# An attention and gated low-rank layer on one core: a new layout of a batch's places, a small softmax that subtracts and sums in ScalarE's exponentials, and a gate that writes its mask itself

## The reference

```
xn   = layernorm(x)
q    = (xn Wq^T + bq) * 0.25            # 16 heads of 16
k, v = split(xn Wkv^T + bkv)            # one k and one v of 16, shared by all heads
attn = softmax(q k^T) v ; y1 = attn Wo^T + bo

g      = one-hot of argmax(xn w_gate)   # 6 experts, the first of equals
tok_e  = A_e B_e                        # A_e 100x16, B_e 16x256
p      = softmax(xn tok_e^T / 16)       # 100 columns, only the chosen expert counts
delta  = ((p[1:] (tok_e Wt^T + wt_b)[1:] + xn) Wd^T + wd_b) * scale
y2     = xn + log(exp(delta))           # a sum of 0 is replaced by a tiny number
out    = x + y1 + y2
```

## Time and profile before

| | |
|---|---|
| median of 3 runs | 1049.19 us (1047.77 to 1050.99) |
| profiled execution | 1037.82 us |
| its span, first to last instruction | 1036.0 us |
| TensorE busy | 892.1 us, 86% |
| VectorE busy | 812.0 us, 78% |
| ScalarE busy | 661.6 us, 64% |
| GpSimd busy | 515.6 us, 50% |
| mean granted TensorE clock | 0.937 of full |

### The profile page before, as it was taken

The page is one execution under the profiler, slowest core; times in us unless marked ns, Lnnn a source line. Parts: engine busy times, 40 slices in busy tenths (PEclk is TensorE's granted clock), DMA queues, the critical chain, the costliest instruction groups (busy, mean ns, idle before and its releaser), DMA issues.

```text
span 1036.0 us, 17715 instructions
## 1 busy us (share of the span) xinstructions
PE 892.1 (86%) x5837; PEld 287.0 (28%) x5837; DVE 812.0 (78%) x1523; ACT 661.6 (64%) x1334; POOL 515.6 (50%) x693
## 2 busy tenths in 40 slices
PE   1368988888999999898998898899899989989986
PEld 0223222322233232222223232223223223222222
DVE  5369898878889896888779787878878888877814
ACT  1003776766677685776667677667757767667882
POOL 1457375555557373555547455555636555532400
PEclk9766999989999998999899999989989999998988
DMA  4224144253524353253525326262533625241121
GB/s 121 60 55 67 56 76 97 74 103 93 87 85 91 105 94 89 82 104 94 95 65 90 102 82 110 87 94 67 90 94 81 114 83 104 61 77 52 54 67 37
DMA packets 128209, 86.56 MB, mean 84 GB/s; under 512 B 60279, under 2 KB 112248, under 8 KB 128120
## 3 DMA queue, kind: packets, MB, share of 16 engines
q1 hardware_dynamic: 128120, 85.43, 36.8%
HBM read 39.28 MB, written 33.54 MB: 70 GB/s over the span
## 4 chain that ended last, share of the span: by engine, by line
PE 53%; DMA 15%; DVE 14%; SPq 6%; ACT 4%; issue 4%; POOL 4%; POOLq 0%
PE pO L358 17%; PE pA L340 12%; DMA o_parts<-OTr 7%; DVE M L768 7%; DMA Lc<-o_parts 6%; PE pB L345 5%; SPq L993 5%; PE pA L483 4%; PE pA L412 3%; PE pA L465 3%; ACT P L585 2%; PE pA L452 2%; PE pA L401 2%; ACT OTr L591 2%; POOL KS L870 2%
## 5 line engine op out<-in xcount | busy, mean ns | idle before, releaser
L768 DVE TENSOR_REDUCE M<-pA 128x1 f32<-128x512 f32 x1024 | 644.6, 678 | 85.0 <-PE pA L340 83.2
L585 ACT ACTIVATE P<-pB 128x512 f32<-128x512 f32 x1002 | 556.7, 600 | 236.4 <-PE pB L345 227.5
L340 PE MATMUL pA<-K,Q 48*128 48x512 f16 x1024 | 342.0, 400 | 78.6 <-DVE M L768 66.9
L345 PE MATMUL pB<-Q,K 50*128 50x512 f16 x1002 | 333.8, 397 | 0.3 <-DVE M L768 0.3
L358 PE MATMUL pO<-P,VK 128*32 128x512 f32 x2048 | 287.1, 634 | 10.1 <-ACT P L585 7.9
L340 PEld LDWEIGHTS pA<-K,Q 48*128 48x128 f16 x1024 | 70.3, 95 | 432.8 <-DVE M L768 374.4
L925 POOL TENSOR_TENSOR On<-Op,Rb 128x512 f32<-128x512 f32 x31 | 39.9, 1287 | 178.2 <-DMA Rb<-l_parts 131.9
L876 POOL CAST Qp<-qf 128x512 f16<-128x512 f32 x32 | 19.5, 609 | 131.4 <-DVE qf L724 131.4
L911 POOL TENSOR_SCALAR Cz<-Cx 128x512 f32<-128x512 f32 x32 | 62.1, 1940 | 30.6 <-ACT Cx L567 30.5
L483 PE MATMUL pA<-wo,On 128*128 128x256 f32 x248 | 71.5, 413 | 3.3 <-DVE RL L781 1.9
L774 DVE RECIPROCAL Rc<-Lc 128x32 f32<-128x32 f32 x31 | 10.9, 353 | 79.5 <-DMA Lc<-o_parts 79.5
(11 more groups left out here) (144 smaller groups left out, 810.3 us busy)
## 6 DMA issues: line engine op xcount, KB each, us to landing
o_parts<-OTr SPq DMA_DIRECT2D x62, 256.0 KB, 2.1
Q<-q_pieces SPq DMA_DIRECT2D x90, 128.0 KB, 5.1
X<-in_x SPq DMA_DIRECT2D x16, 512.0 KB, 3.9
q_pieces<-Qp SPq DMA_DIRECT2D x32, 256.0 KB, 2.3
out<-OUT SPq DMA_DIRECT2D x32, 256.0 KB, 3.2
Op<-o_parts SPq DMA_DIRECT2D x31, 256.0 KB
Rb<-l_parts SPq DMA_DIRECT2D x31, 256.0 KB
K<-KS SPq DMA_DIRECT2D x96, 16.0 KB, 1.8
```

The costliest lines, as they stand in the source:

```text
L340: e.matmul(bank1("ab", t)[:, :], Q16[r:r + 48, b % 2, h, 128 * s:128 * s + 128], K16[r:r + 48, b % 3, :], start=True, stop=True).then_inc( ...
L345: e.matmul(bankB(t)[:, :], K16[r:r + 50, b % 3, 128 * i:128 * i + 128], Q16[r:r + 50, b % 2, :, 32 * hh:32 * hh + 32], start=True, stop=Tr ...
L585: e.activation(P[:, u % PR, :], bankB(u + LB)[:, :], ACT.Exp, scale=alpha).then_inc(S("e"))
L768: e.tensor_reduce(M[:, t // 32 % 2, t % 2, t % 32 // 2:t % 32 // 2 + 1], bank1("ab", t)[:, :], AX, ALU.max, negate=True).then_inc(S("mx"))
```

## The change

Three things are changed together. First, SLOT has other places, and with them go three Q buffers instead of two, other DMA shapes for Q and K (k's 16 rows come out of the projection twice, so that one copy carries two of the three pieces), the evictions qf on ScalarE instead of VectorE, and another start: the first batch's tokens are transposed by TensorE, ScalarE makes the high pieces of the weights and issues the first batch's K copies, and the first Q reads go out in two separate places. Second, the small softmax: VectorE writes the negated maximum, four exponentials of 100 columns read the scores in PSUM with it as bias and write their sums; Sd and the sum on VectorE are gone, and the factor 1/16 is in UK's scale. Third, the gate's last comparison writes the 384 mask elements itself; `oh` and GpSimd's cast are gone.

```diff
 SLOT = {
-    "root": -91.4, "refine": -90.2, "norm": -87.2, "pieces": -84.2, "xtd": -74.2,
-    "residual": 2.3, "q0": -57, "qe0": -55.4, "qs0": -53.8, "qw0": -50.2, "uk": -53, "uke": -51.4, "ks": -50.2,
...
+    "root": -91.4, "refine": -90.2, "norm": -87.2, "ph": -82.4, "pl": -79, "xtd": -66.2,
+    "residual": 9.1, "q0": -53, "qe0": -51.4, "qs0": -47.5, "qw0": -45, "uk": -49, "uke": -47.4, "ks": -45.2,
...
-PARTH = {"lr": 66.2, "or": 66.3, "rec": 68.8, "lw": 69.4, "rb": 72.2, "on": 78.3}
+PARTH = {"lr": (82.2, 114.2), "or": (82.3, 114.3), "rec": (88.8, 120.8), "lw": (89.6, 121.4), "rb": (92.4, 124.4),
+         "on": (98.2, 130.3)}
...
-        Q16 = sb("Q16", [128, 2, H, T // 2], F16)
+        Q16 = sb("Q16", [128, 3, H, T // 2], F16)
...
-            "ab": lambda t: (S("mx"), t + 1), "s": lambda b: (S("sd"), b + 1),
+            "ab": lambda t: (S("mx"), t + 1), "s": lambda b: (S("es"), 4 * b + 4),
...
+                for c in range(2):
+                    if due(f"xt{c}", n) is not None:
+                        w.wait_ge(*before2(f"xt{c}", 0))
+                        w.wait_ge(S("id"), 4)
+                        for i in range(4):
+                            w.wait_ge(S("xn"), i + 1)
+                            mm = e.transpose(bank2(f"xt{c}", 0)[:, 128 * i:128 * i + 128], XN[:, i, 128 * c:128 * c + 128],
+                                             idf[:, :])
+                        mm.then_inc(S("xtp"))
...
+                if due("kd", n) == 0:
+                    w.wait_ge(S("kl"), 1)
+                    w.wait_ge(S("kc"), 2)
+                    for a in range(2):
+                        e.dma_start(K16[64 * a:64 * a + 32, 0, :], KS[96:128, 0, :]).then_inc(S("kd"), 16)
+                        e.dma_start(K16[64 * a + 32:64 * a + 48, 0, :], KS[96:112, 1, :]).then_inc(S("kd"), 16)
+
+                for g in range(2):
+                    if (b := due(f"qe{g}", n)) is not None:
+                        w.wait_ge(S(f"q{g}"), b + 1)
+                        w.wait_ge(S("bqs"), 1)
+                        w.wait_ge(S(f"ql{g}"), b)
+                        e.activation(qf[:, g, :], bank1(f"q{g}", b)[:, :], ACT.Identity, scale=scl[:, 5:6],
+                                     bias=bq_s[:, g:g + 1]).then_inc(S(f"qe{g}"))
...
-                    w.wait_ge(S("sd"), b + 1)
+                    w.wait_ge(S("sm"), b + 1)
                     w.wait_ge(S("en"), b)
-                    e.activation(Es[:, :, :], Sd[:, :, :], ACT.Exp, scale=C ** -0.5).then_inc(S("es"))
+                    for i in range(4):
+                        e.activation(Es[:, i, :], bank1("s", b)[:, NL * i:NL * i + NL], ACT.Exp, bias=smx[:, i:i + 1],
+                                     accum_out=sL[:, i:i + 1]).then_inc(S("es"))
...
-                    w.wait_ge(S("mk"), b)
-                    e.tensor_tensor(oh[:, :, :], gw[:, :, :], bc(gm2[:, :], NE), ALU.is_equal).then_inc(S("oh"))
+                    w.wait_ge(S("mkd"), 16 * b)
+                    w.wait_ge(S("mk1"), 1)
+                    e.tensor_tensor(mk[:, :, 0:ER].rearrange("p i (e r) -> p i e r", r=NR), bc(gw[:, :, :], NR),
+                                    bc(bc(gm2[:, :], NE), NR), ALU.is_equal).then_inc(S("mk"))
...
-                    e.tensor_reduce(smx[:, :], s4, AX, ALU.max).then_inc(S("sm"))
-                    w.wait_ge(S("sm"), b + 1)
-                    w.wait_ge(S("es"), b)
-                    e.tensor_tensor(Sd[:, :, :], s4, bc(smx[:, :], NL), ALU.subtract).then_inc(S("sd"))
+                    w.wait_ge(S("es"), 4 * b)
+                    e.tensor_reduce(smx[:, :], s4, AX, ALU.max, negate=True).then_inc(S("sm"))
...
-                if (b := due("qread", n)) is not None:
-                    if b >= 2:
-                        w.wait_ge(S("b"), 64 * (b - 1))
...
+                if (b := due("qread", n)):
+                    w.wait_ge(S("qw_0"), 32 * (b + 1))
+                    w.wait_ge(S("qw_1"), 32 * (b + 1))
+                    if b > 2:
+                        w.wait_ge(S("b"), 64 * (b - 2))
+                    for a in range(2):
+                        for p, pieces in ((0, 2), (32, 1)):
+                            e.dma_start(Q16[64 * a + p:64 * a + p + 16 * pieces, b % 3, :, :],
+                                        qd[b % 2, :, 0:pieces, :, 256 * a:256 * a + 256]
+                                        .rearrange("h k d t -> (k d) h t")).then_inc(S(f"qr_{b % 2}"), 16)
```

More of the change, by code:

```diff
@@ L23 @@
 ER = NE * NR
-U0, K0, V0, WC = C, C + ER, C + ER + D, C + ER + D + 32
-UKW = ER + D
+U0, K0, V0, WC = C, C + ER, C + ER + 2 * D, C + ER + 2 * D + 32
+UKW = ER + 2 * D
 LN_EPS = 1e-5
@@ L119, in slots @@
                 put(name, 16 * g + slot + 4 * (g >= 4 * NB - 4), g)
-        if g % 2 and g < 4 * NB - 2:
-            for name, slot in PARTH.items():
-                put(name, 16 * g + slot + 4 * (g >= 4 * NB - 4), g // 2)
+    for nh in range(2 * NB - 1):
+        for name in PARTH:
+            put(name, 64 * (nh // 2) + (PARTH_LAST[name] if nh == 2 * NB - 2 else PARTH[name][nh % 2]), nh)
     return at
@@ L703, in _ @@
                     e.tensor_tensor(rstd[:, :], y4[:, :], y0[:, :], ALU.mult).then_inc(S("ry"))
-                if due("pieces", n) == 0:
-                    for k in range(2):
-                        w.wait_ge(S("xh0"), k + 1)
-                        e.tensor_tensor(XP[:, 2 * k:2 * k + 2, 1, :], XN[:, 2 * k:2 * k + 2, :],
-                                        XP[:, 2 * k:2 * k + 2, 0, :], ALU.subtract).then_inc(S("xl0"))
+                for c in range(2):
+                    if due(f"xl{c}", n) is not None:
+                        w.wait_ge(S("xh0"), c + 1)
+                        e.tensor_tensor(xT[:, 0, :, 1, c, :], bank2(f"xt{c}", 0)[:, :].rearrange("p (i t) -> p i t", t=128),
+                                        xT[:, 0, :, 0, c, :], ALU.subtract).then_inc(S("xl"))
                 if (b := due("uke", n)) is not None:
@@ L717, in _ @@
                                     ALU.mult, ALU.add).then_inc(S("uke"))
-                for g in range(2):
-                    if (b := due(f"qe{g}", n)) is not None:
-                        w.wait_ge(S(f"q{g}"), b + 1)
-                        w.wait_ge(S("bqs"), 1)
-                        w.wait_ge(S(f"ql{g}"), b)
-                        e.tensor_scalar(qf[:, g, :], bank1(f"q{g}", b)[:, :], scl[:, 5:6], bq_s[:, g:g + 1],
-                                        ALU.mult, ALU.add).then_inc(S(f"qe{g}"))
+                if due("qs0", n) == 0:
+                    w.wait_ge(S("qe0"), 1)
+                    e.tensor_copy(Qp[:, 0, 0, :], qf[:, 0, :]).then_inc(S("qh0"))
+                    w.wait_ge(S("qh0"), 1)
+                    e.tensor_tensor(Qp[:, 0, 1, :], qf[:, 0, :], Qp[:, 0, 0, :], ALU.subtract).then_inc(S("ql0"))
                 if (b := due("gate", n)) is not None:
@@ L872, in _ @@
                 for g in range(2):
-                    if (b := due(f"qs{g}", n)) is not None:
+                    if (b := due(f"qs{g}", n)) is not None and b + g:
                         w.wait_ge(S(f"qe{g}"), b + 1)
-                        w.wait_ge(S(f"qw_{g}"), 16 * b)
+                        w.wait_ge(S(f"qw_{g}"), 32 * b)
                         e.tensor_copy(Qp[:, g, 0, :], qf[:, g, :]).then_inc(S(f"qh{g}"))
@@ new lines, in _ @@
+                        for k in range(2):
+                            e.dma_start(qd[b % 2, 8 * g:8 * g + 8, k], Qp[:, g, k, :]).then_inc(S(f"qw_{g}"), 16)
+                for half, name in enumerate(("qra", "qrb")):
+                    if due(name, n) is not None:
+                        w.wait_ge(S(f"qw_{half}"), 32)
+                        for a in range(2):
+                            for p, pieces in ((0, 2), (32, 1)):
+                                e.dma_start(Q16[64 * a + p:64 * a + p + 16 * pieces, 0, 8 * half:8 * half + 8, :],
+                                            qd[0, 8 * half:8 * half + 8, 0:pieces, :, 256 * a:256 * a + 256]
+                                            .rearrange("h k d t -> (k d) h t")).then_inc(S(("qf", "qr_0")[half]), 16)
```

163 lines of the change are left out of this document (75 added, 88 removed), and 8 rows, old and new, of the table SLOT.

## The result

The changed kernel takes 936.15 us (median of 4 runs, 935.8 to 937.19), the kernel before 1048.48 us on the same chip (4 runs, 1039.02 to 1050.99): a ratio of 0.8945, 95% interval 0.8889 to 0.9001. The profiled execution took 935.8 us. Forecast: 928, range 903 to 972. The kernel before varies from run to run (1025 to 1056 us on one chip of the experiments), and every ratio with its interval compares the fast runs of the two kernels only.

A forecast was written before the change was run, and what follows sets the result against it. No engine was saturated; VectorE's `rec` waits for the row sums and clock falls cost time. Span 1036.0 - 96.5 (batches) - 15 (start) - 1 (tail) = 923.5; 925 profiled with 1.8 around it, plus 3: 928 us, range 903 to 972.

The forecast's parts named there:

- The stall and the clock: VectorE's `rec` waits for Lc vanish, 4.65 us per batch (65.1 in all); TensorE's clock stops falling, 27 us.
- The Q reads: SyncE's queue: `qread` moves to ten places ahead of `ow`; the reads need 8 us or nine places, so clear it.
- VectorE: VectorE's evictions and small operations: net -2.7 us busy per batch, counted as -1.0, bounds 0 and -2.
- ScalarE: ScalarE gains two `qf` and four exponentials for one Es: +2.7 us busy per batch, counted +0.7, bounds 0 and 2.7.
- over 15 us of such waits: Sign that the forecast is wrong: TensorE's waits on ScalarE for a bank grow past 15 us.
- ScalarE becomes the bound: Rival, chance 0.12: ScalarE frees q0's, q1's and the small softmax's banks late, 0.9 us each; period 55, 966 us.
- The period: Time per batch: 57.3 - 4.65 - 1.0 + 0.7 = 52.3 us; fourteen batches -96.5 us.
- Start and tail: Start: mask ready near 30.2, -15 us, bounds -8 and -22. Tail: last batch's places hardly move, -1 us.
- The clock did not fall again: Rival, chance 0.10: TensorE's clock still falls through short idle times; 955 us as often as now, 987 once every batch.
- Slower by On, the guard and `dlog0`: Rival, chance 0.03: `on` waits for Rb ahead of GpSimd's guard, ScalarE's `dlog0` behind; up to 10.4 us a batch, 1074.
- Part of the `rec` wait stays: Rival, chance 0.05: one `rec` in a batch still waits 2 us and the clock falls as now, 983 us.
- Better: Case, chance 0.04: VectorE's whole 2.7 us per batch count, 900 us.

The follow-up runs named there:

- Experiment 1: Kernel before with `rec`, `lw`, `rb` and `on` four places later: 1044.67 us, ratio 1.0136.
- experiment 2: Kernel before with `rec`, `lw`, `rb`, `on` and also `o0` four places later: 965.99 us, ratio 0.934.
- experiment 4: Changed kernel with Q's reads back at place 45.8, still with three Q buffers: 935.26 us, ratio 0.8987.
- experiments 6: Changed kernel with the old small softmax and the old gate, so the layout alone: 921.22 us, ratio 0.8935.
- experiment 7: Changed kernel with one small part undone: old softmax alone 927.13 us, ratio 0.8959; old gate alone 930.65 us, ratio 0.8989.
- experiment 8: Changed kernel, three variants: one of three d-projection products left out, 922.73 us; row maxima over 448 of 512 columns, 928.12; `qf` back on VectorE, 944.38.
- experiment 3: Changed kernel with `rec`, `lw` and `rb` four places earlier: 939.86 us, ratio 0.9112.
- experiment 5: Kernel before with only the new small softmax and the gate that writes the mask, old layout: 1036.15 us, ratio 1.0027.

## Why the prediction was right, and where it was not

**The stall and the clock (step: minus 4.65 per batch, minus 27 for falls).** The state forecast came about: no `rec` wait in the fourteen batches, clock 1.00 for all 742.7 us, batches near 53. The mechanism held for Lc; the attribution did not hold for the rest. The prediction took `rec` to be the stall and gave its disappearance to `rec`'s four places and to Q's. Experiment 1 shows that a later `rec` by itself only hands the stall to `o0`; experiment 2 that `o0`'s move is needed with it in that kernel: from place 3.0 to 7.2 there, to 7.0 in the change (131 to 135 in SLOT), which the prediction does not name. A wait was costed as if removing it ended the matter, when it stood at the head of a chain of two DMA round trips whose other end was due at a fixed place. The sizes were off as well, in opposite ways: the `rec` waits counted 65.1 us, and TensorE's idle time, all causes together, fell by 53.3; the clock counted 27 us, called its upper bound, and TensorE's busy time fell by 32.8.

**The Q reads (step: "`qread` moves from 45.8 to 38.2 ... so they now clear it").** The effect is there, Lc 2.1 us behind `ow`; the cause named is wrong. The new place gives the same order as the old one (experiment 4), and the reads come earlier because they no longer wait 3.6 us a batch for a buffer. The prediction knew of that wait and did not count its end.

**VectorE (step: -2.7 busy, -1.0 counted).** Busy went from 49.1 to 46.8 us in the batches shown, -2.3. What the small softmax and the gate's mask contributed to the period has the wrong sign: +0.75 together (experiments 6 and 7), and some 3 us in batch 0. The gate's error lies in a duration: `oh` was taken at 764 ns, its mean before, so that the mask in its stead seemed free. In the new layout `oh` takes 182 ns and the mask 558. The 764 belonged to `oh`'s neighbour, below.

**ScalarE (step: +2.7 busy, +0.7 counted).** It has 42.7 us per batch where 43.9 were forecast: +1.5 for +2.7. By the lengths of the added instructions, the ones that read the sums included, it would be 2 x 0.77 + 4 x (0.35 + 0.21) - 0.54 = +3.2; rows of neighbours overlap, and busy time counts such a stretch once. `qf` took 772 ns (800 forecast), an exponential 347 (400). By the Trainium skill's sum (ScalarE: Activation LUTs, What ACT_TABLE_LOAD costs) they would have been an estimated 799 and 362; the trace agrees within 30 ns. What was not foreseen is the instruction behind each exponential. The groups of the changed kernel, and one of the four pairs with what TensorE does behind it:

```profile
L574 ACT ACTIVATE qf<-pA,bq_s,scl 128x512 f32<-128x512 f32 x32 | 24.7, 772 | 19.5 <-PE pA L426 19.5
L596 ACT ACTIVATE Es<-pA,smx 128x100 f32<-128x100 f32 x64 | 21.0, 347 | 2.2 <-DVE smx L788 2.2
L596 ACT ACTIVATION_READ_ACCUMULATOR Es<-pA,smx 128x1 f32 x64 | 13.5, 211 | 0.0
```

```profile
558.22 0.34 ACT L596 ACTIVATE Es<-pA,smx 128x100 f32<-128x100 f32 x1
558.45 0.20 ACT L596 ACTIVATION_READ_ACCUMULATOR Es<-pA,smx 128x1 f32 x1
...
559.50 1.10 ACT L627 ACTIVATE P<-pB 128x512 f32<-128x512 f32 x2
...
559.68 0.39 PE L344 MATMUL pA<-K,Q 48*128 48x512 f16 x1 [0.48 <-ACT Es L596]
```

The group holds ScalarE from 558.22 to 559.50, 1.3 us where Es took 0.54, and it holds the bank of `s` too: before, VectorE's subtraction freed that bank; now the last exponential does, and TensorE waits for it once in every batch, 14 times, 6.8 us in all (the 10.9 us of its weight loads in the same list lie over the same moments, 558.90 to 559.68 and 559.20 to 559.68 here). The prediction's sign for the rival, over 15 us of such waits, did not appear. That is the mechanism of the rival "ScalarE becomes the bound" for one of its three banks, and 0.49 us a batch is the likely place of the softmax's 0.4 us, as the wait comes and goes with the four exponentials (experiment 7). The term of +0.7 per batch held in size against the two parts together, but the gain of 1.0 set against it did not come from them. Of the 1.8 us between experiment 2's batch and the layout's (54.1 and 52.3), `qf`'s move to ScalarE has 0.6 by experiment 8; the other 1.2 are not separated: the third Q buffer, fewer issues, and many other places moved together.

**The period.** Forecast 52.3, measured 53.05; fourteen batches -86.0 us instead of -96.5. The miss is the 0.75 above, nearly to the digit, since the layout alone gave 52.3. The rest agrees in part by luck: two attributions in the sum were wrong.

**Start and tail.** -15 forecast, -14.7 measured, which already holds the 3 us that the two small parts cost in batch 0; no run takes the parts of the new start one by one. The second batch's projection at 47.37 lies within the 46 to 49 forecast, the mask was ready at 29.4, near the 30.2. The tail gave -1.3 for -1. The median lies 0.35 us above the profiled execution; 3 had been allowed for.

**The rivals.** The clock did not fall again: 14 batches with their short waits for a bank ran at 1.00, which the Trainium skill's rule of the depth-cycling queue (TensorE: Matmul & The Clock Gate, A second HAM failure mode: psum-queue depth-cycling) would not lead one to expect; no run here shows that failure. Slower by On, the guard and `dlog0`: On waited 3.1 us in all for Rb, ScalarE's Cz 0.2 us for the guard's operand. Part of the `rec` wait stays: none did, and in experiment 3, where 12.8 us stayed, it cost 3.7 us and one fall of the clock, not the 55 of the rival. *Better*: its sum is off, 928 - 14 x 1.7 is 904, not 900, and so that case lay inside the range.

## What to carry to other kernels

Before a wait is costed as removable, follow its result to the last consumer that has a fixed place in some engine's order: in a chain of DMA round trips every fixed end must move, or the stall only changes its name (1044.67 us with one end moved, 965.99 with both). A new place is a change only if it passes another piece of work on the same engine. In a queue that issues when a semaphore allows, look for what the semaphore waits on, a buffer, not for where the instruction stands. And once TensorE sets the pace, work taken off VectorE is worth a fraction of its length (0.4 us for 4.0, 0.6 for the two `qf` of 1.6), while an instruction that holds a bank longer costs what TensorE waits for it; the part of a change that looked like its arithmetic gain was 15 us of loss.

## What the runs showed of the hardware

A sum taken along with an exponential is not free: each comes with an instruction of its own on ScalarE, 211 ns for one column, behind an exponential of 347. The rows overlap, and four such pairs start 0.32 us apart. The two P behind them, 0.62 us each, start 0.48 us apart; with the same overlap of 0.14 us exponentials without a sum would start some 0.21 us apart, so the sum costs about 0.1 us each, an estimate.

A small operation of VectorE can depend on its neighbour on GpSimd. In one batch of the kernel before, the four operations of 24 elements ahead of `oh` ran in 170 to 180 ns each (the last of them is shown), and `oh`, of the same size, in 1.12 us:

```profile
605.22 0.18 DVE L737 TENSOR_REDUCE gm<-gw 128x4 f32<-128x24 f32 x1
605.24 1.27 POOL L913 TENSOR_TENSOR Cx<-Cx,Cz 128x512 f32<-128x512 f32 x1
605.43 1.12 DVE L740 TENSOR_TENSOR oh<-gw,gm 128x24 f32<-128x24 f32 x1
```

It began 0.19 us into a GpSimd operation with two operands and ended 0.04 us behind it. The trace has all cases: of the 16 `oh` of this kernel the nine that began within this GpSimd operation took 1.00 to 1.29 us, each ending 0.04 us behind it; the seven others took 0.18, one of them although it overlapped: it had begun 0.04 us before. In experiments 1 and 2, whose other places made 15 of the 16 `oh` begin beside GpSimd's one-operand Cz instead, all took 0.18 us, and in experiment 5, at the old place, the mask itself had six of 16 at 1.3 to 1.6 us, the rest at 0.56. The groups of experiments 2 and 5:

```profile
L740 DVE TENSOR_TENSOR oh<-gw,gm 128x24 f32<-128x24 f32 x16 | 2.9, 182 | 0.6
```

```profile
L743 DVE TENSOR_TENSOR mk<-gw,gm 128x384 bf16<-128x384 f32 x16 | 14.4, 902 | 0.6
```

No run moved only the GpSimd operation, but the same instruction with and without that neighbour, within one kernel and across four, makes another cause unlikely. In this record the operation that began first ran at its own length.
